# Four fused decoder layers on one core: the mixing of the streams moved from VectorE to ScalarE and GpSimd, and the down projection woven with the first maxima

## The reference

```
xn = layernorm(x)
x  = x + attention(xn) * silu(feed_forward(xn))
```

```
H_res = sinkhorn(logits, 50 iterations)          # a 4x4 matrix for each token
x_mixed[t, i, :] = sum_j H_res[t, i, j] * x[t, j, :]
y_distributed[t, i, :] = y[t, :] * H_post[t, i]
out = x_mixed + y_distributed
```

## Time and profile before

| | us |
|---|---|
| median of 3 runs | 1273.21 |
| profiled execution | 1270.83 |
| its span | 1268.8 |
| PE busy (share) | 1050.2 (83%) |
| DVE busy | 834.3 (66%) |
| ACT busy | 565.0 (45%) |
| POOL busy | 328.4 (26%) |

### The profile page before, as it was taken

How to read it: one execution, slowest core, us unless ns; L and a number is a source line. 1 busy time by engine, 2 the same in 40 slices (tenths; PEclk the granted TensorE clock), 3 DMA queues, 4 the chain that set the end, 5 groups by cost and what they waited for, 6 DMA issues and landing times.

```text
span 1268.8 us, 19873 instructions
## 1 busy us (share of the span) xinstructions
PE 1050.2 (83%) x7480; PEld 444.8 (35%) x7480; DVE 834.3 (66%) x1475; ACT 565.0 (45%) x797; POOL 328.4 (26%) x516
## 2 busy tenths in 40 slices
PE   2889999897898997865535639899899988999998
PEld 2434444343333444531211302223233234434344
DVE  6322222001786884798997999888978787876874
ACT  2533333100565664502123335858645767354671
POOL 2145444001776311000002136360000042011230
PEclk9989999998698998786657758999999999999999
DMA  8421220001321011020000032140012111220200
GB/s 306 143 73 55 72 75 25 1 1 49 89 64 35 26 37 60 14 63 22 16 0 1 27 102 74 48 148 28 20 35 69 51 44 39 64 76 26 69 17 34
DMA packets 54899, 69.72 MB, mean 55 GB/s; under 512 B 9526, under 2 KB 43444, under 8 KB 54800
## 3 DMA queue, kind: packets, MB, share of 16 engines
q1 hardware_dynamic: 50828, 58.57, 14.7%
q0 software_dynamic: 3984, 9.98, 2.8%
HBM read 49.45 MB, written 18.82 MB: 54 GB/s over the span
## 4 chain that ended last, share of the span: by engine, by line
DVE 30%; PE 30%; issue 4%; ACT 4%; POOL 3%; DMA 3%; SPq 1%; ACTq 0%; DVEq 0%; POOLq 0%
DVE w_mx L1320 14%; PE w_banks L667 8%; PE w_po L1250 7%; PE w_banks L1230 4%; PE w_banks L1202 3%; DVE w_region L1933 2%; ACT w_pr L1270 2%; PE w_banks L1190 2%; PE w_banks L1584 2%; DVE w_region L1893 1%; DVE w_region L1930 1%; DVE w_region L1928 1%; DVE w_region L1926 1%; DMA w_ks<-stack_scratch 1%; DVE w_region L1924 1%
## 5 line engine op out<-in xcount | busy, mean ns | idle before, releaser
L1320 DVE TENSOR_REDUCE w_mx<-w_banks 128x2 f32<-128x1024 f32 (+3 forms) x352 | 368.6, 1086 | 94.0 <-PE w_banks L1202 92.6
L1270 ACT ACTIVATE w_pr<-w_banks 128x1024 f32<-128x1024 f32 (+1 forms) x312 | 304.2, 1014 | 214.3 <-PE w_banks L1230 201.9
L1308 POOL TENSOR_SCALAR_AFFINE_SELECT w_pr<-w_pr 128x512 f32<-128x512 f32 (+1 forms) x184 | 107.8, 591 | 396.1 <-ACT w_pr L1270 396.1
L1230 PE MATMUL w_banks<-w_qs,w_ks 49*128 49x512 f16 (+7 forms) x832 | 125.4, 346 | 42.9 <-DVE w_mx L1320 30.3
L1202 PE MATMUL w_banks<-w_ks,w_qs 48*128 48x512 f16 (+7 forms) x832 | 139.4, 351 | 25.1 <-DVE w_mx L1320 11.3
L1250 PE MATMUL w_po<-w_pr,w_vz 128*17 128x512 f32 (+7 forms) x1152 | 142.8, 533 | 17.1 <-DVE w_vz L909 6.7
L78 PE MATMUL f_pp<-xt,sl_region 128*128 128x512 f16 x672 | 149.2, 383 | 2.4 <-POOL sl_region L504 2.4
L480 DVE TENSOR_TENSOR sl_region<-sl_region,f_pp 128x512 f32<-128x512 f32 x28 | 19.3, 688 | 120.3 <-ACT sl_region L495 120.3
L78 PEld LDWEIGHTS f_pp<-xt,sl_region 128*128 128x128 f16 x672 | 65.2, 99 | 83.8 <-issue 5.6
L1230 PEld LDWEIGHTS w_banks<-w_qs,w_ks 49*128 49x128 f16 (+1 forms) x832 | 36.0, 97 | 147.1 <-issue 58.3
L1190 PE MATMUL w_banks<-mask_half,ident_half 64*128 64x128 bf16 (+1 forms) x768 | 64.7, 248 | 17.9 <-DMA w_ks<-stack_scratch 8.6
(11 more groups left out here) (221 smaller groups left out, 1478.9 us busy)
## 6 DMA issues: line engine op xcount, KB each, us to landing
stack_scratch<-sl_region SPq DMA_DIRECT2D x102, 128.0 KB
w_qs<-stack_scratch SPq DMA_DIRECT2D x96, 96.0 KB, 2.3
sl_region<-in_L_gu SPq DMA_DIRECT2D x14, 512.0 KB
w_stage<-in_L_w POOLq DMA_DIRECT2D x36, 128.0 KB, 2.4
sl_region<-in_L_down SPq DMA_DIRECT2D x14, 256.0 KB
stack_scratch<-p_qk SPq DMA_DIRECT2D x24, 128.0 KB
w_ks<-stack_scratch SPq DMA_DIRECT2D x32, 96.0 KB, 2.5
bw_stage<-in_L_w SPq DMA_DIRECT2D x4, 640.0 KB, 10.1
```

What stands on the lines that cost most here:

```text
L1230: mm = pe.matmul(g.banks.pair_at(f)[:, half, at:at + T - q0], g.ks[base:base + self.rows + 1, k_slot, k_place, j * P:(j + 1) * P], g.qs[ba ...
L1270: act.activation(g.probs.at(self.pr_fill[s])[:, :, 0:width], g.banks.pair_at(self.s_fill[s])[:, :, 0:width], ACT.Exp, scale=self.a.scale). ...
L1308: pool.affine_select(out=diagonal, in_=diagonal, compare_op=ALU.is_ge, fill=0.0, base=0, pattern=pattern, channel_multiplier=-1).then_inc( ...
L1320: dve.tensor_reduce(out, g.banks.pair_at(self.m_fill[m])[:, :, 0:heads * keys].rearrange("q h (p k) -> q h p k", k=keys), AX.X, ALU.max).t ...
```

## The change

**The down projection** loses its phase. A new stage `Down` does the same matmuls four at a time (11 ticks for each tile of tokens) and the same Silu. `down_and_maxima` runs a block ahead of the weave, with an order of its own (`FIRST_TURNS`), in which the stage Down (`d`) alternates with the loads of attention 00 for groups 0 to 2 (`q4`), their 18 maxima units (`m`) and 3 turns (`t`). The block has programs for PE, ACT, DVE and SP, none for POOL. `clear_semaphores` and its barrier still come behind it, and then the weave. The PSUM banks, the signals and four small SBUF tiles are created earlier for this.

**The mixing** of the streams leaves DVE. For each of the 16 pairs of tile and stream j of a batch ACT makes the 4 products of 128x128 into one of two tiles `h_scaled`, and POOL adds the 128x512 tile to `h_om`. ACT's product k waits for POOL's sum k-2. The two tiles lie where `h_xp` and `h_xpt` lie, so the first product on streams of s1 (its `pre` ticks, on DVE) waits until all sums of s0 are done.

**The order** TURNS is a new one throughout.

```
+        finish(dt, wd)                       # in place of phase d0
...
+FIRST_TURNS = "q4 d6 " + "m1 d5 " * 6 + "t1 " + "m1 d5 " * 6 + "t1 d2 " + "m1 d3 " * 6 + "t1 d3"
 TURNS = """
-    w10 m5 q m2 q2 l m t m q m3 e m e t m e m e m2 v e m v e q e v t w2 q e o m2 v m e m v m e2 o m w v e2 w v m w e
...
+    w12 q w17 e5 v e2 v2 m q e m e m e o v m2 e v m e m v l m2 v t m e2 q v m2 o2 e2 v2 e t e v e m2 v m o2 e2 m v e
...
+class Down(Stage):
...
+    def pe(self, pe, t):
+        i, k = divmod(t, self.parts)
...
+        mm = partial(pe, self.g.banks.at(self.fills[i]), lambda part, c: self.gated[:, part, c, i * P:(i + 1) * P],
+                     lambda part, c: self.w[:, part, c, :], range(self.chunks), PRODUCTS, 4 * k, 4 * k + 4)
...
+    def scale(self, act, k):
+        g, (i, j) = self.g, divmod(k, self.N)
+        if k == 0:
+            act.wait_ge(self.done.sem, self.done.at + 13)
+        if k > 1:
+            act.wait_ge(self.mixed.sem, self.mixed.at + k - 1)
+        else:
+            act.wait_ge(self.kept.sem, self.kept.at + 1)
+        for m in range(self.N):
+            op = act.activation(g.h_scaled[k % 2][:, m * P:(m + 1) * P], self.xn[:, i, j * P:(j + 1) * P], ACT.Copy,
+                                scale=g.h_mix[:, self.b, i, m * self.N + j:m * self.N + j + 1])
+        op.then_inc(self.scaled.sem, 1)
...
+                if self.earlier is not None:
+                    dve.wait_ge(self.earlier.mixed.sem, self.earlier.mixed.at + NI * n)
...
-            for s in range(n):
-                o = g.h_om[:, i % 2, s * P:(s + 1) * P]
-                if j > 0:
-                    dve.wait_ge(self.mixed.sem, self.mixed.at + i * 16 + (j - 1) * n + s + 1)
-                dve.scalar_tensor_tensor(out=o, in0=self.xn[:, i, j * P:(j + 1) * P],
-                                         scalar=g.h_mix[:, b, i, s * n + j:s * n + j + 1], in1=o,
-                                         op0=ALU.mult, op1=ALU.add).then_inc(self.mixed.sem, 1)
+    def pool(self, pool, t):
+        k = t - self.mix_at - 1
+        if not 0 <= k < NI * self.N:
+            return
+        g, i = self.g, k // self.N
+        if k % self.N == 0:
+            pool.wait_ge(self.posted.sem, self.posted.at + i + 1)
+        else:
+            pool.wait_ge(self.mixed.sem, self.mixed.at + k)
+        pool.wait_ge(self.scaled.sem, self.scaled.at + k + 1)
+        pool.tensor_tensor(g.h_om[:, i % 2, :], g.h_om[:, i % 2, :], g.h_scaled[k % 2], ALU.add).then_inc(self.mixed.sem, 1)
...
+def down_and_maxima(nc, top, g, stack_dram, gated, w):
...
+    merge({"d": [all_of(down)], "q": [some_of(first.stacks, 0, SLOTS + 1)], "m": [some_of(first.maxima, 0, SLOTS * first.n_m)],
+           "t": [some_of(first.turns, 0, SLOTS)]}, FIRST_TURNS, order, g.emitted, g.banks)
+    with nc.Block() as block:
...
+        first_layer(nc, g, ins, x_tiles, by_chunk, lambda gated, w: down_and_maxima(nc, top, g, stacks[0], gated, w))
         clear_semaphores(nc)
         weave(nc, top, g, ins, out, stacks, by_chunk, sign_region, sign_qkv, sign_o)
...
+    g.h_scaled = view(region, 4096, (D,), F32), view(region, 4608, (D,), F32)
```

More of the change, by code:

```diff
@@ L1996, in some_of, with rest_of @@
     return stage, range(first, last)
+def rest_of(stage, emitted):
+    return stage, [t for t in stage.ticks if (stage, t) not in emitted]
 class Shared:
@@ new lines, in split_rows, with done @@
+    def split_rows(name, dst, chunks=KC):
+        return [(by_chunk(name, chunks)[:, c, :], dst[:, 0, c, :], dst[:, 1, c, :]) for c in range(chunks)]
+    def done(stage):
+        return stage.normed, stage.groups
+    a00 = g.first
+    a01 = Attend(g, h[0], 1, vz(0, 1), att(1), stacks[0], None, a00)
+    split1 = Split(g, split_rows("L0_wo", wo) + split_rows("L1_w", w1)
+                   + split_rows("L1_wo", wo1, 2) + split_rows("L1_w24", w24) + [(ins["L1_wb"], wb[:, 0], wb[:, 1])])
+    o00 = Outward(g, h[0], 0, lambda part, c: wo[:, part, c, :], o_rows[:, 0, :], att(0), sl[:, 0], done(a00), None,
+                  [split1.done(), small.done()])
@@ new lines, in weave @@
+    n11 = Normalise(g, 1, (o01.added, NI), sl[:, 1])
+    p11 = Project(g, h[1], 1, lambda part, c, cols: w1[:, part, c, cols], col1, v_row1, vz(1, 1), n11, stacks[1], [])
+    a11 = Attend(g, h[1], 1, vz(1, 1), att(1), stacks[1], p11, a10)
+    s1 = Streams(g, 1, sl[:, 1], w24, wb, base24[:, :], gate[:, :], n11, [])
+    s1.begins_after = [(n11, n11.ticks[-1])]
+    balance = Balance(g, (s0, s1))
+    s1.earlier = s0
+    o10 = Outward(g, h[1], 0, lambda part, c: wo1[:, part, c, :], o_rows[:, 1, :], att(0), sl[:, 0], done(a10),
+                  s0.ready(), [])
@@ new lines, in weave, with _ @@
+    merge(strands, TURNS, order, emitted, g.banks)
+    with nc.Block() as block:
+        @block.tensor
+        def _(pe):
+            pe.wait_ge(po_zeroed.sem, po_zeroed.at + 1)
+            for stage, t in order:
+                stage.pe(pe, t)
+        @block.scalar
+        def _(act):
+            for stage, t in order:
+                stage.act(act, t)
+        @block.vector
+        def _(dve):
+            dve.memset(g.po[:, :], 0.0).then_inc(po_zeroed.sem, 1)
+            for stage, t in order:
+                stage.dve(dve, t)
+        @block.gpsimd
+        def _(pool):
+            for stage, t in order:
+                stage.pool(pool, t)
+        @block.sync
+        def _(sp):
+            for stage, t in order:
+                stage.sp(sp, t)
+            for stage in (o30, o31):
+                sp.wait_ge(stage.stored.sem, stage.stored.at + 16 * NI)
@@ L2291, in lay_out @@
+    nc.clear_and_free_semaphores(list(g.signals.sems.values()))
+    nc.all_engine_barrier()
 def lay_out(v):
```

345 lines of the change are left out of this document (161 added, 184 removed).

## The result

The changed kernel took 1313.67 us (median of 4 runs, 1307.47 to 1315.7) against 1272.28 for the kernel before (4 runs, 1271.23 to 1274.51): a ratio of 1.0315, 95% interval 1.0276 to 1.0354. It is slower by 41 us, or 3%. The forecast was 1309 with a range of 1284 to 1327. The profiled execution took 1307.47 us, with a span of 1305.8, 37.0 more than the span before. It is the fastest of the four and lies 6 us under their median, so the trace accounts for 37 of the 41 us; where the other 4 lie it can't show.

What follows compares the result with a forecast made beforehand. PE bounds the down projection and the stretch to Balance, then DVE, a chain, and both; POOL's queue sets the weave's start. 13 + 31 - 5 - 3 = +36 us gives 1307 against the profiled execution, 1309 against the median; range 1284 to 1327.

Steps and rivals of the forecast that it cites:

- (1): Down projection: 18 maxima units put between PE's matmuls lengthen it, +13 us until the weave begins.
- (2): Weave's start: all 29 pieces of split 1 precede POOL's first mask, 33.2 us more, less 2 us work done: +31 us.
- (3): First values to Balance: fewer waits for masks, units moved behind Balance's start, four reductions added on DVE: -5 us.
- the rival: First values to Balance: the order wins the time back, PE running without idle time; 1292 us, chance 20%.
- (4): Mixing moved from DVE to ACT and POOL: +2 us for s0, -5 us for s1, together -3 us.
- (5): Layers 2 and 3 reordered, split 3 one block of 32 pieces on POOL: 0, give or take 8 us.
- The first mask: Sign at the weave's start: POOL's first mask comes 56 to 60 us behind the barrier.
- the idle PE: Sign at the weave's start: PE, ACT and DVE idle for some 50 us before POOL's first mask.
- the low clock: Sign at the weave's start: granted clock at the lower level when PE resumes.
- the stretch to Balance: Sign: from the first values to Balance's first step about 200 us.
- POOL free of the barrier: Rival at line 351's barrier: POOL begins split 1 during the down projection, pieces do not hold masks; 1257 us, chance 6%.
- Held sums: Rival in the mixing: POOL's sums wait beside DVE's two-SBUF-input instructions, one 7 us hold a batch; 1319 us, chance 12%.

Runs made afterwards that it cites:

- the run with ten pieces ahead: Changed kernel with 10 of split 1's 29 pieces at the weave's start, 19 spread before exponents 7 to 46: 1277.74 us, 1.0042 against the kernel before.
- the pair with three pieces ahead: Changed kernel with three pieces of split 1 ahead, 26 spread before exponents 5 to 47: 1262.76 us with the new mixing, 1268.47 us with DVE's.

## Why the prediction was right, point by point

Forecast +36 us on the span, measured +37.0; the mechanism that carried it, POOL's queue ahead of the first mask, is shown by the run with ten pieces ahead. That the sum came out within 1 us is luck all the same: the steps are off by -2.5, -0.6, +0.8, -2.0, +7.9 and -3.1 us, and these nearly cancel. By its steps:

(1) *Maxima inside the down projection*: +13, measured +10.5. The maxima's own matmuls took what was foretold. PE's time by their two lines (L1210 the masks, L1222 the scores) in this stage of the changed kernel is

```profile
232.00:317.00 85.00, 5.84 (x72) 2.11 (x72) 0.98 0.03 9
232.00:317.00 85.00, 6.29 (x48) 2.43 (x48) 0.98 0.03 9
```

or 0.67 us for each of the 18 units, against 0.65. But in part they lie beside the down matmuls: PE's busy time in the whole stage rose only by 10.3 us, from 74.21 to 84.49. The list of PE's waits between 232 and 317 us has none for DVE.

(2) *The order of POOL's queue*: 33.2 us foretold for the stretch, 32.6 measured; POOL's pitch held (57.4 us from its first issue to the first values, 56.84 measured). The 2 us taken off for work done by then, which made it +31, belong to the next stretch, from which that work is gone.

(3) *From the first values to Balance*: the -5 was made of 3.7 for the masks' waits and 5 for the units moved out, less 4 added inside Balance. With the 2 us of (2) that is -10.7 up to Balance and +4 in it; measured -9.9 and +2.0. The size was right, the way to it in part not. The waits for masks did go, but others came in their place: PE's idle time stayed (206 - 183.6 = 22.4 before, 196 - 173.3 = 22.7 after), so the order won nothing back from it, as argued against the rival. What shrank is PE's work in the stretch, by 10.3 us where 7 were foretold: 47 matmuls fewer, and a granted clock of 0.96 against 0.92, which had no term. The runs don't part the two.

(4) *The mixing*: -3, measured +4.9, the step that failed. The sum compared two ways of mixing and left out that the order of this stretch changes as well. The run with DVE's mixing in the new order parts the two: from the last step ahead of the mixing to the first maxima it takes 78.4 us (782.43 - 704.00), where the kernel before takes 74.1 and the changed kernel 79.0. So the new order costs 4.3 us here, the term that is missing, and the new mixing 0.6 rather than -3. In the pair with three pieces ahead it is 79.6 with DVE's mixing and 78.3 with the new one, so the mixing is worth about nothing in this stretch, give or take a us. That is the balance of a loss on s0, 4.5 us in the new order (29.4 against 24.9 to the second Silu) where +2 was foretold, and a gain of 3.9 between that Silu and the maxima (49.7 against 53.6) where 5 was. Part of the loss is POOL's sum: 1.27 us, where the row with one float16 operand gave 1.16, so that POOL and not ACT set the pace; at 1.35 for each of eight sums that is 1.2 us more than the 9.6 foretold.

(5) *The rest*: 0 give or take 8, measured -3.1. It too is made of two effects. The new order leaves a part of s1's mixing behind the first maxima of attention 20, 24 of 64 instructions where DVE does it. Done by DVE, it splits the maxima, and the stretch takes 528.3 us, 3.3 more than in the old order, where the mixing was over by then. Done by ACT and POOL it takes 521.9, 6.4 less. The prediction said that what DVE saves otherwise it saves in waiting time; that holds only up to the first maxima.

*Signs and range.* The first mask (56.0 us behind POOL's first issue), the down projection of 85 us, the idle PE (53 us), the low clock and the stretch to Balance (196.6 us) came as foretold. From Balance's end to the first maxima 79.0 us passed instead of about 70, which is step (4) again. The upper end of the range was added up wrongly: 1309 with 6, 4 and 10 is 1329, and with the reordering's 5 taken back 1334, not 1327; and 60 + 20 + 12 is 0.92 before any share of the rest, not 0.90. The measured time lies inside either range.

*The rivals.* The order winning back PE's idle time did not happen (point 3). POOL free of the barrier did not either: it waited 87.19 us for line 351. Held sums were seen in one place, and small. POOL and DVE in the changed kernel, by line for the three sums from 745 to 755 us, and DVE's timeline beside them:

```profile
L1932 POOL TENSOR_TENSOR w_region<-w_region x3: 1267/1461/1595, 748.0 to 751.2; 128x512 f32<-128x512 f32 x3
```

```profile
747.03 0.68 DVE L1046 TENSOR_TENSOR x_res<-x_res,att 128x512 f32<-128x512 f32 x1
...
748.35 1.64 DVE L1046 TENSOR_TENSOR x_res<-x_res,att 128x512 f32<-128x512 f32 x1
```

The first two of the three sums took 1.46 and 1.60 us instead of 1.27, while DVE had additions with two SBUF inputs; and the one at 748.35 took 1.64 us, where the other three of line 1046 here took 0.68, so DVE lost more than POOL. The traces with three, ten and no pieces ahead show the same place again, with a longest sum of 1.60 us, and in the three traces of the new mixing in the old order none of the 32 sums took more than 1.272. This agrees with the page "GPSIMD Engine Reference" (Key points) of the Trainium skill, that the two engines contend for their SBUF interfaces in such instructions; here POOL lost 0.2 and 0.3 us and DVE 1.0. A hold of 7 us like that in the earlier trace rows did not come; the long DVE run that stood beside it is what the change removed.

What the prediction had not asked is what each part would do by itself. In the old order the down projection's weaving costs 8.5 us and the mixing 22; with no piece ahead of the first mask the whole change is 13 us faster than the kernel before, and moving the pieces gives 6 without any of the change. That 6 was measured with three pieces ahead; the kernel before with none was not run, so how the 13 divide is not shown.

## What to carry to other kernels

In an order written out by hand, look at what stands ahead of the first instruction that another engine waits for: 29 pieces in POOL's queue, where ten had stood, cost 33 us, and moving them alone turned a loss of 41 us into a gain of 13. Before crediting a change with such a gain, make the same move in the kernel before: there it gave 6. Work moved to an idle engine enters an in-order queue; it is free only if nothing that others wait for stands behind it, and the same mixing cost 22 us in one order and won 4 to 7 in another. When a change has several parts, try each alone and each removed, because they did not add up here.

## What the runs showed of the hardware

A POOL addition of 128x512 all in float32 took 1.261 to 1.271 us in all 32 sums of the run with the mixing alone, 0.11 more than with one float16 operand; back to back such sums, each waiting for the one before, start 1.36 us apart (8 in 10.77 us, the last of which takes 1.27). Beside a DVE addition with two SBUF inputs they took 1.46 and 1.60 us, and the DVE addition 1.64 instead of 0.68. The three first DMAs that POOL issued in the weave landed at different speeds: the first cast came 2.6 us behind the issue in the changed kernel, 3.3 in the kernel before, and 5.4 and 5.2 in the two runs with the stage Down in the old order; no run tells why.
